# Edge weights of layer 1, made beside the edges of layer 0, stored in rows of their own and loaded by layer 1

## The chip, the cores and the metric

The kernel runs on one core of a Trainium2 chip. Everything is 32-bit float. The metric is the device time in microseconds. A core has five engines that run side by side, each with its own queue of instructions: PE (TensorE, matmuls), ACT (ScalarE), DVE (VectorE), POOL (GpSimd) and SP (SyncE, which only issues DMAs here). They wait for one another through semaphores.

## The reference

Two graph layers follow one another on 50000 nodes with 160 features (64 scalars, 32 vectors of 3) and 25000 edges. A layer maps the features of each edge's source node, multiplies them with weights made from the edge's own attributes, sums the results by target node, maps them once more, and adds a residual and a layer norm. Cut to the parts that matter:

```
def layer0(x, a, src, dst, edge_attr_4, edge_attr_64):
    hid = silu(edge_attr_64 @ fc_w1 / 8)
    w = hid @ fc_w2 / 8                       # 25000 x 224
    es, ev = h_s[src], h_v[src]               # lin1 of x, gathered
    mid = products of w, es, ev, edge_attr_4
    agg = segment_sum(mid, dst)
    ...
def layer1(x, a, edge_attr_16, edge_attr_4, src, dst):
    h = silu(edge_attr_16 @ (Wfc1 / 4))
    w = h @ (Wfc2 / 8)                        # 25000 x 192
    ...
x = layernorm(x + layer0(x, node_vec1, src, dst, edge_attr_4, edge_attr_64))
x = layernorm(x + layer1(x, node_vec1, edge_attr_16, edge_attr_4, src, dst))
```

The `w` of layer 1 depends on `edge_attr_16` and weights alone, not on layer 0.

## The kernel before

The kernel has four stages: edges of layer 0, nodes of layer 0, edges of layer 1, nodes of layer 1. In an edge stage the edges go in 98 pairs of tiles (256 edges a pair), in a node stage the nodes go in 98 groups of 512. The edge sums are added to a table in DRAM by indirect DMAs of POOL (scatters, L500), and source rows come by indirect DMAs of POOL (gathers, L483).

Each engine has its own program for a stage. `run_stages` gives each a list of steps with a lag, and in round i a step with lag n works on pair i - n, in the order of the list. So the order on an engine is written out by hand. In layer 0's edges:

- PE: first_map (lag 1), hidden (0), edge_weights (1), turn_x (0), second_map (3), turn_mid (2), sum_pair (5).
- ACT: copy_z (0), copy_h (1), hidden_act (0), copy_xT (0), copy_message (3), copy_midT (2), copy_sums (5).
- DVE: message vectors (4), scaled attributes (0), comparisons (2), products (1) and the choice of rows (2, 3).
- POOL: gather(k), then scatter(k - 8). A scatter waits for the copied sums of its pair and for the landing of the scatter of the pair before (L493).
- SP: the attributes, the row of targets, and the clearing of layer 1's table, which waits for a scatter to land.

In layer 1's edges PE and ACT also make the self connection of a group of nodes (nodes1a and b, turn1a and b), and SP loads `x1` (320 KB) and stores `base_rows` (320 KB) each round. The edge weights of a pair are made by hidden (L599, attributes times fc1), hidden_act (L763, Silu) and edge_weights (L616 in layer 0, L618 in layer 1), and read out of PSUM by DVE's products.

A wait that matters is in `copy_message`: ACT copies the message of pair j only when PE has summed pair j - 2, since the message buffer has two halves. As copy_message has lag 3 and sum_pair lag 5, it waits for the last matmuls of the same round.

## Time and profile before

| what | value |
|---|---|
| three runs | 2071.84, 2082.07 and 2080.49 us, median 2080.49 |
| the profiled execution | 2057.88 us, its span 2055.1 us |
| busy in the span | PE 1436.3, DVE 1438.8, ACT 1062.9, POOL 1474.8 us |
| mean granted clock of PE | 0.878 of full speed |
| DMA | 439.92 MB, mean 214 GB/s |

The page shows the span in 40 slices of 51 us. In its rows the four stages can be told apart: the two edge stages are slices 3 to 14 and 22 to 34 with 130 to 170 GB/s, the node stages are those with 300 to 400 GB/s, where the DMA engines are busy nearly all the time. The first two slices clear the tables (385 and 430 GB/s). PEclk is the clock that PE was granted, in tenths of full speed; busy shares are tenths as well. An idle gap in an engine's timeline stands in brackets ahead of what ended it; "issue" means that the profile has no name for it.

### The profile page before, as it was taken

Reading aid. Unit: us, or ns where it says so; the run is one execution under the profiler, and the core shown is the slowest. Engines: PE = TensorE matmul, PEld = TensorE weight load, DVE = VectorE, ACT = ScalarE, POOL = GpSimd, SP = SyncE. Lnnn points to the kernel's source line nnn. Section 1 sums busy time; section 2 is a strip of 40 time slices with the busy share of each in tenths; the row PEclk is TensorE's granted clock in tenths of the full one; section 3 lists DMA queues with packets and bytes.
Section 4 is the critical chain, followed back from the end, with each engine's and each line's share of the span. In section 5 each row is a group of like instructions: output and inputs, shape, how many; then the busy total and the mean of one; then the engine's idle time right before and its main releaser. Section 6 shows DMA issues by size and latency. Waiting matters only on the chain.

```text
span 2055.1 us, 48034 instructions
## 1 busy us (share of the span) xinstructions
PE 1436.3 (70%) x10424; PEld 1275.1 (62%) x10424; DVE 1438.8 (70%) x5759; ACT 1062.9 (52%) x3600; POOL 1474.8 (72%) x1923
## 2 busy tenths in 40 slices
PE   5078888788888848888876998999989999300000
PEld 4067777677777737676755888888888888300000
DVE  5067777677777719999983665666656666289998
ACT  3034444444444418999973554554545454146676
POOL 3067888777787647888873777777777777468887
PEclk9589999999999979999997999999999999755555
DMA  9967666676666749999954777777777777499997
GB/s 385 430 151 134 133 137 136 135 132 136 136 135 134 178 101 340 339 337 338 340 208 138 166 167 166 167 170 167 164 162 170 161 169 162 80 362 402 400 399 294
DMA packets 253883, 439.92 MB, mean 214 GB/s; under 512 B 33424, under 2 KB 131152, under 8 KB 250576
## 3 DMA queue, kind: packets, MB, share of 16 engines
q1 hardware_dynamic: 152304, 311.47, 45.1%
q0 software_dynamic: 75264, 67.79, 24.3%
q10 hardware_dynamic: 26208, 59.65, 7.5%
q14 instruction: 91, 0.75, 0.1%
q8 instruction: 16, 0.26, 0.0%
HBM read 235.50 MB, written 203.27 MB: 214 GB/s over the span
## 4 chain that ended last, share of the span: by engine, by line
PE 26%; issue 21%; POOL 13%; ACT 13%; DVE 9%; DMA 6%; SPq 4%; another core or an unknown queue 3%; ACTq 3%; DVEq 1%; POOLq 0%
ACT y L845 9%; POOL table L500 7%; POOL xg L483 5%; DVE stats L1081 3%; SPq L374 3%; DMA table<-sums,row_all 3%; PE ps L679 3%; DVE res L1042 3%; PE ps L660 2%; PE ps L641 2%; PE ps L627 2%; PE ps L643 2%; ACTq L857 2%; PE ps L669 2%
## 5 line engine op out<-in xcount | busy, mean ns | idle before, releaser
L500 POOL DMA_INDIRECT table<-sums,row_all x392 | 630.9, 1609 | 316.4 <-issue 131.2
L782 ACT COPY msg<-ps 128x192 f32<-128x192 f32 (+1 forms) x196 | 57.4, 293 | 680.9 <-PE ps L660 495.8
L845 ACT ACTIVATE y<-res,norm 128x160 f32<-128x160 f32 x756 | 330.3, 507 | 125.8 <-POOL norm L536 69.0
L991 DVE SCALAR_TENSOR_TENSOR x1g<-ps,a_all,x1g 128x160 f32<-128x160 f32 x392 | 132.3, 379 | 200.2 <-PE ps L680 95.3
L483 POOL DMA_INDIRECT xg<-in_x_rows,src_all x196 | 201.8, 1029 | 59.6 <-issue 58.7
L483 POOL DMA_INDIRECT xg<-x_rows,src_all x196 | 195.8, 999 | 64.3 <-issue 58.5
L641 PE MATMUL ps<-weights,midT 128*128 128x128 f32 (+1 forms) x784 | 164.0, 293 | 86.9 <-DVE msg L951 84.8
L946 DVE TENSOR_TENSOR pe<-ps,ea_all 128x192 f32<-128x192 f32 x196 | 69.8, 356 | 185.1 <-ACT msg L782 99.8
L1081 DVE BATCH_NORM_STATS2 stats<-res 128x6 f32<-128x160 f32 x784 | 196.0, 311 | 3.8 <-issue 0.3
L641 PEld LDWEIGHTS ps<-weights,midT 128*128 128x128 f32 x784 | 127.2, 204 | 94.9 <-issue 87.7
L534 POOL TENSOR_TENSOR half_rstd<-var,minus_half 128x8 f32<-128x8 f32 x98 | 165.0, 1683 | 14.2
L643 PE MATMUL ps<-weights,midT 128*128 128x96 f32 x784 | 154.9, 281 | 0.0
L714 PE MATMUL ps<-weights,xzT 128*128 128x160 f32 x784 | 134.0, 313 | 17.7 <-DVE tab L1018 17.7
L591 PE MATMUL ps<-ident,xg 128*128 128x128 f32 x392 | 88.6, 309 | 70.3 <-ACT xz L769 40.2
L679 PEld LDWEIGHTS ps<-weights,xzT 128*128 128x128 f32 x784 | 108.7, 193 | 46.0 <-issue 31.0
L599 PE MATMUL ps<-attrT,weights 128*128 128x128 f32 x392 | 91.5, 316 | 64.4 <-DMA attrT<-in_attrT 43.9
L835 ACT ACTIVATE res<-tab,a_all 128x64 f32<-128x64 f32 x392 | 104.5, 336 | 52.7 <-DVE tab L1018 36.5
L607 PE MATMUL ps<-weights,xgT 128*128 128x128 f32 x784 | 122.4, 280 | 9.2 <-ACT xgT L776 4.7
L679 PE MATMUL ps<-weights,xzT 128*128 128x128 f32 x784 | 122.8, 279 | 8.4 <-issue 3.8
L643 PEld LDWEIGHTS ps<-weights,midT 128*128 128x128 f32 x784 | 128.1, 205 | 0.0
L627 PE MATMUL ps<-ident,mid 128*128 128x128 f32 x784 | 126.7, 287 | 0.0
L714 PEld LDWEIGHTS ps<-weights,xzT 128*128 128x128 f32 x784 | 110.5, 191 | 24.7 <-DMA xzT<-in_xzT 17.9
(115 smaller groups left out, 4465.4 us busy)
## 6 DMA issues: line engine op xcount, KB each, us to landing
tab<-table SPq DMA_DIRECT2D x98, 384.0 KB, 5.0
table<-zeros SPq DMA_DIRECT2D x24, 1536.0 KB
table<-zeros SPq DMA_DIRECT2D x98, 324.0 KB
tab<-table SPq DMA_DIRECT2D x98, 324.0 KB, 5.4
xzT<-in_xzT SPq DMA_DIRECT2D x98, 320.0 KB, 4.9
x1g<-x_rows SPq DMA_DIRECT2D x98, 320.0 KB
base_rows<-x1g SPq DMA_DIRECT2D x98, 320.0 KB
x1g<-base_rows SPq DMA_DIRECT2D x98, 320.0 KB, 4.9
```

The source lines that it names most:

```text
L483: pool.indirect_dma_start(out=xg[j % RING][:, t, 0:width], out_offset=None, in_=rows, in_offset=bass.IndirectOffsetOnAxis(ap=src_all[:, at ...
L500: pool.indirect_dma_start(out=table[l], out_offset=bass.IndirectOffsetOnAxis(ap=row_all[:, at:at + 1], axis=0), in_=sums[j % 4][:, t, 0:W] ...
L534: tt(half_rstd[:, :], var4[:, :], minus_half[:, :], ALU.pow).then_inc(s_rstd, 2)
L607: mm(h_ps[:, t, 0:M], xgT[u][:, t, :], lin1_m[l][:, :], start=True, stop=True)
L627: last = turn(midT_ps[:, 2 * c + t, :], mid[u][:, t, c * P:(c + 1) * P], ident[:, :])
L641: mm(o_ps[l][:, t, 0:SO + V], midT[u][:, t, :], mapA[l][:, :], start=t == 0, stop=not L["cross"], skip_group_check=True)
L643: last = mm(o_ps[l][:, t, SO + V:SO + 4 * V], midT[u][:, 2 + t, :], mapB[l][:, :], start=False, stop=not L["cross"], skip_group_check=True)
L679: mm(n1_ps[:, t, 0:M], xT[v][:, q], self_m[1][:, :], start=True, stop=True)
L714: mm(o[:, t, 0:160], xT[u][:, t * P:(t + 1) * P], self_m[0][:, :], start=True, stop=True)
L845: last = nc.scalar.activation(y[u][:, t, :], res[u][:, t, :], ACT.Identity, scale=rstd[u][:, t:t + 1], bias=shift[u][:, t:t + 1])
L991: last = stt(x1g[v][:, 2 * b + t, :], n1_ps[:, t, :], a, x1g[v][:, 2 * b + t, :], ALU.mult, ALU.add)
L1081: last = nc.vector.bn_stats(stats[u][:, t, :], res[u][:, t, :])
```

## The change

Layer 1's edge weights are now made in layer 0's edge stage, pair by pair. PE gets a matmul of the 16 attributes (`hid1T_ps`) at the head of turn_x and two matmuls for the weights at the head of edge_weights. ACT gets hidden1_act (Silu) and copy_weights1 (PSUM to SBUF, lag 2, right behind copy_z). SP loads both sets of attributes in layer 0 and stores each pair's weights, 128 x 384 floats, to `w1_rows` in DRAM. In layer 1, hidden, hidden_act and edge_weights are gone, and SP loads the weights of each pair in the place where it loaded the attributes; DVE's products wait for that load. Buffers of the node stages (`tab`, `y`) hold the new tiles, and the clearing of attrT on DVE between the layers is gone.

```diff
+        w1_rows = dram("w1_rows", (NP * P, 2 * 192))
...
+        w1_made, w1_read = [[flat(tab2[h + u // 4][:, :, :])[:, u % 4 * 384:(u % 4 + 1) * 384].rearrange("p (t c) -> p t c", t=2)
+                             for u in range(RING)] for h in (0, 2)]
...
+                def store_weights1(j, m, u):
+
+                    wait_count(sp, s_w1store[u], landed(j - 4, u % 4, 4))
+                    sp.sem_inc(s_sptick, 1)
+                    sp.wait_ge(s_w1, j + 1)
+                    sp.sem_inc(s_sptick, 1)
+                    sp.dma_start(w1_rows[bass.ds(m * P, P), :], w1_made[u].rearrange("p t c -> p (t c)")).then_inc(s_w1store[u], 16)
+
+                def load_weights1(j, m, u):
+
+                    wait_count(sp, s_mid, j - 7)
+                    sp.sem_inc(s_sptick, 1)
+                    wait_count(sp, s_w1load[u], landed(j - 4, first_of(u % 4, 4), 4))
+                    sp.sem_inc(s_sptick, 1)
+                    sp.dma_start(w1_read[u].rearrange("p t c -> p (t c)"), w1_rows[bass.ds(m * P, P), :]).then_inc(s_w1load[u], 16)
...
                 if l == 1:
-                    sp.wait_ge(s_attr0, 1)
                     for u in range(4):
                         sp.wait_ge(s_store[u], stored(NG, u))
-                run_stages(sp, base, NP, 10, [(0, load_attr), (0, load_dst_row)] +
-                           ([(0, clear_table0), (8, clear_table1)] if l == 0 else [(4, store_base), (0, load_x1)]), RING)
+                if l == 0:
+                    run_stages(sp, 0, NP, 10, [(0, load_attr), (0, load_dst_row), (0, clear_table0), (5, store_weights1),
+                                               (8, clear_table1)], RING)
+                    for u in range(4):
+                        sp.wait_ge(s_w1store[u], stored(NP, u))
+                else:
+                    run_stages(sp, NP, NP, 10, [(0, load_weights1), (0, load_dst_row), (4, store_base), (0, load_x1)], RING)
...
+                    if l == 0:
+                        pe.wait_ge(s_attr[u], landed(j, u, RING, 32))
+                        wait_count(pe, s_hid1sb, j)
+                        mm(hid1T_ps, fc1[1][0:2 * LAYERS[1]["R"], :], attr1T[u], start=True, stop=True).then_inc(s_hid1, 1)
...
                     wait_count(pe, s_mid, j)
-                    if l == 0:
-                        for t in range(2):
-                            q = slice(t * H, (t + 1) * H)
-                            last = mm(w_ps[0][:, t, :], hidT[u][q, :], fc2[0][q, :], start=True, stop=True)
-                    else:
-                        last = mm(w_ps[1].rearrange("p t c -> p (t c)"), hidT[u][:, :], fc2[1][:, :], start=True, stop=True)
+                    pe.wait_ge(s_hid1sb, j + 1)
+                    wait_count(pe, s_w1, j)
+                    for t in range(2):
+                        mm(w1_ps[:, t, :], hid1T[u], fc2[1][:, t * 192:(t + 1) * 192], start=True, stop=True)
+                    for t in range(2):
+                        q = slice(t * H, (t + 1) * H)
+                        last = mm(w_ps[:, t, :], hidT[u][q, :], fc2[0][q, :], start=True, stop=True)
                     last.then_inc(s_wd, 1)
...
+                def hidden1_act(j, m, u):
+
+                    act.wait_ge(s_hid1, j + 1)
+                    act.wait_ge(s_xgT, j + 1)
+                    wait_count(act, s_wd, j - 1)
+                    nc.scalar.activation(hid1T[u], hid1T_ps, ACT.Silu).then_inc(s_hid1sb, 1)
+
+                def copy_weights1(j, m, u):
+
+                    act.wait_ge(s_mid, j + 1)
+                    wait_count(act, s_w1store[u], landed(j - RING, u % 4, 4))
+                    copy(w1_made[u], w1_ps).then_inc(s_w1, 1)
...
-                    dve.wait_ge(s_wd, j + 1)
+                    if l == 0:
+                        dve.wait_ge(s_wd, j + 1)
+                    else:
+                        dve.wait_ge(s_w1load[u], landed(j, first_of(u % 4, 4), 4))
```

The instructions themselves, first PE in the edge stage of layer 0, from the head of a round (L607, first_map) to the head of second_map. Before (`hidT` is the hidden layer, `xg` the gathered rows, `midT` the turned products):

```order
L607 MATMUL ps<-weights,xgT 128x128 [waits hidden_copied,h_copied,xg_turned_copied]
L607 MATMUL ps<-weights,xgT 128x128
L608 MATMUL ps<-weights,xgT 128x2x32
L599 MATMUL ps<-attrT,weights 128x128 [waits hidden_copied,attr_loaded0]
L616 MATMUL ps<-weights,hidT 128x224 [waits products_ready]
L616 MATMUL ps<-weights,hidT 128x224
L591 MATMUL ps<-ident,xg 128x128 [waits xg_turned_copied,z_gathered_together,rows_gathered0]
L591 MATMUL ps<-ident,xg 128x128
L592 MATMUL ps<-ident,xz 64x128
L641 MATMUL ps<-weights,midT 128x128 [waits message_vectors_ready,message_scalars_ready,products_turned_copied]
```

After (line numbers have moved: first_map is L653, hidden L644, turn_x L636; `y` holds the hidden layer of layer 1 in L662 and its attributes in L634; L662 are the new weights, L665 the old ones):

```order
L653 MATMUL ps<-weights,xgT 128x128 [waits hidden_copied,h_copied,xg_turned_copied]
L653 MATMUL ps<-weights,xgT 128x128
L654 MATMUL ps<-weights,xgT 128x2x32
L644 MATMUL ps<-attrT,weights 128x128 [waits hidden_copied,attr_loaded0]
L662 MATMUL ps<-weights,y 128x192 [waits edge_weights1_copied,hidden1_copied,products_ready]
L662 MATMUL ps<-weights,y 128x192
L665 MATMUL ps<-weights,hidT 128x224 x2
L634 MATMUL ps<-y,weights 128x128 [waits attr_loaded0,xg_turned_copied,hidden1_copied,z_gathered_together,rows_gathered0]
L636 MATMUL ps<-ident,xg 128x128 x2
L637 MATMUL ps<-ident,xz 64x128
L688 MATMUL ps<-weights,midT 128x128 [waits message_vectors_ready,message_scalars_ready,products_turned_copied]
```

Three matmuls stand in the round more, and the first of the edge weights waits for `edge_weights1_copied`, ahead of turn_x.

ACT in the edge stage of layer 0, a round from copy_message on. Before (`msg` is the message, `sums` the pair's sums, `xz` the part of the gathered rows that is brought together):

```order
L782 COPY msg_1<-ps 128x2x96 [waits pair_summed,second_map_done]
L788 COPY midT<-ps 128x512 [waits second_map_done,products_turned]
L790 COPY midT<-ps 96x256
L797 COPY sums<-ps 128x384 [waits pair_summed]
L769 COPY xz<-xg 128x64 [waits xg_turned,rows_gathered1]
L755 COPY hs<-ps 128x2x160 [waits products_ready,hidden_done,h_done]
L757 COPY hs<-ps 128x2x64
L763 ACTIVATE hidT<-ps 128x128 [waits edge_weights_done,hidden_done]
L775 COPY xgT<-ps 128x256 [waits h_done,xg_turned]
```

After (L823 is copy_weights1, into the buffer `tab`; L817 is hidden1_act):

```order
L842 COPY msg_0<-ps 128x2x96 [waits pair_summed,second_map_done]
L848 COPY midT<-ps 128x512 [waits second_map_done,products_turned]
L850 COPY midT<-ps 96x256
L857 COPY sums<-ps 128x384 [waits pair_summed]
L829 COPY xz<-xg 128x64 [waits xg_turned,rows_gathered0]
L823 COPY tab<-ps 128x384 [waits products_ready]
L802 COPY hs<-ps 128x2x160 [waits products_ready,hidden_done,h_done]
L804 COPY hs<-ps 128x2x64
L810 ACTIVATE hidT<-ps 128x128 [waits edge_weights_done,hidden_done]
L835 COPY xgT<-ps 128x256 [waits h_done,xg_turned]
L836 COPY xgT<-ps 64x128
L817 ACTIVATE y<-ps 128x128 [waits edge_weights_done,xg_turned,hidden1_done]
```

The copy of the new weights stands between `xz` and `hs`, the second Silu behind the copies of the turned rows.

PE in the edge stage of layer 1, from first_map to turn_x. Before (L618 are the edge weights, L679 and L680 the self connection):

```order
L607 MATMUL ps<-weights,xgT 128x128 [waits hidden_copied,h_copied,xg_turned_copied]
L607 MATMUL ps<-weights,xgT 128x128
L608 MATMUL ps<-weights,xgT 128x2x32
L599 MATMUL ps<-attrT,weights 128x128 [waits hidden_copied,attr_loaded0]
L618 MATMUL ps<-weights,hidT 128x384 [waits products_ready]
L679 MATMUL ps<-weights,xzT 128x128 [waits self_connection_added,nodes_turned_copied]
L679 MATMUL ps<-weights,xzT 128x128
L680 MATMUL ps<-weights,z1T 128x2x32
L591 MATMUL ps<-ident,xg 128x128 [waits xg_turned_copied,z_gathered_together,rows_gathered0]
```

After:

```order
L653 MATMUL ps<-weights,xgT 128x128 [waits h_copied,xg_turned_copied]
L653 MATMUL ps<-weights,xgT 128x128
L654 MATMUL ps<-weights,xgT 128x2x32
L726 MATMUL ps<-weights,xzT 128x128 [waits self_connection_added,nodes_turned_copied]
L726 MATMUL ps<-weights,xzT 128x128
L727 MATMUL ps<-weights,z1T 128x2x32
L636 MATMUL ps<-ident,xg 128x128 [waits xg_turned_copied,z_gathered_together,rows_gathered0]
```

The matmul of the hidden layer and that of the edge weights are gone with their waits; the self connection (now L726) follows first_map.

## Rows read from the trace of the kernel before

**Rows 1.** The page, part 1: engine, busy us (share of the span) and instructions.

```profile
PE 1436.3 (70%) x10424; PEld 1275.1 (62%) x10424; DVE 1438.8 (70%) x5759; ACT 1062.9 (52%) x3600; POOL 1474.8 (72%) x1923
```

**Rows 2.** Stretches: us, engines' busy us, PEclk, DMA share, GB/s.

```profile
108.00:754.00 646.00, 524.43 (x3697) 463.08 (x3697) 452.61 (x2252) 260.98 (x928) 498.50 (x373) 0.93 0.66 132
...
1131.00:1790.00 659.00, 590.21 (x4592) 543.81 (x4591) 399.14 (x1589) 322.01 (x1303) 488.93 (x372) 0.97 0.73 161
1790.00:2055.00 265.00, 0.00 (x0) 0.00 (x0) 233.50 (x896) 165.68 (x378) 200.72 (x541) 0.50 0.95 362
```

**Rows 3.** Timeline of POOL, layer 0: start, us, instruction [idle before].

```profile
403.30 1.63 POOL L500 DMA_INDIRECT table<-sums,row_all  x1 [0.30 <-issue]
...
407.12 1.02 POOL L483 DMA_INDIRECT xg<-in_x_rows,src_all  x1 [0.30 <-issue]
...
409.73 1.62 POOL L500 DMA_INDIRECT table<-sums,row_all  x1 [0.31 <-issue]
```

**Rows 4.** Waits of POOL, 117 to 707: us in total, times, longest.

```profile
POOL table L500 <- issue: 58.4, 172, 0.8
...
POOL table L500 <- ACT sums L797: 3.5, 3, 2.2
POOL table L500 <- DMA table<-sums,row_all: 2.8, 3, 1.1
```

**Rows 5.** Waits of POOL, 1138 to 1740.

```profile
POOL table L500 <- issue: 67.3, 163, 1.2
POOL xg L483 <- issue: 52.7, 173, 0.3
POOL table L500 <- DMA table<-sums,row_all: 19.1, 13, 2.7
POOL table L500 <- ACT sums L797: 1.9, 2, 1.1
```

**Rows 6.** Timeline of PE, layer 0, one round.

```profile
408.18 0.49 PE L660 MATMUL ps<-msg,same 128*128 128x192 f32 x2
...
410.41 0.44 PE L591 MATMUL ps<-ident,xg 128*128 128x128 f32 x2 [0.27 <-issue]
...
410.79 0.39 PE L641 MATMUL ps<-weights,midT 128*128 128x128 f32 x2
...
413.42 0.49 PE L660 MATMUL ps<-msg,same 128*128 128x192 f32 x2
413.74 0.61 PE L607 MATMUL ps<-weights,xgT 128*128 128x128 f32 x4
```

**Rows 7.** Timeline of ACT, layer 0, the same round.

```profile
408.76 0.32 ACT L782 COPY msg<-ps 128x192 f32<-128x192 f32 x1 [2.50 <-issue]
...
409.72 0.50 ACT L797 COPY sums<-ps 128x384 f32<-128x384 f32 x1
410.09 0.26 ACT L769 COPY xz<-xg 128x64 f32<-128x64 f32 x1
```

**Rows 8.** Timeline of PE, then POOL, at the start and end of layer 0's pairs.

```profile
115.01 0.53 PE L660 MATMUL ps<-msg,same 128*128 128x192 f32 x2
...
117.36 1.83 POOL L500 DMA_INDIRECT table<-sums,row_all  x1 [2.22 <-ACT sums L797]
...
728.72 1.56 POOL L500 DMA_INDIRECT table<-sums,row_all  x1 [2.73 <-ACT sums L797]
```

**Rows 9.** Timeline of PE, layer 1.

```profile
1411.46 0.44 PE L599 MATMUL ps<-attrT,weights 128*128 128x128 f32 x2
1411.74 0.81 PE L618 MATMUL ps<-weights,hidT 128*128 128x384 f32 x2
1412.47 0.68 PE L679 MATMUL ps<-weights,xzT 128*128 128x128 f32 x4
```

**Rows 10.** Timeline of POOL, the first scatter of layer 1.

```profile
1130.87 1.62 POOL L500 DMA_INDIRECT table<-sums,row_all  x1 [24.83 <-ACT sums L797]
```

More of the change, by code:

```diff
@@ L205, in program, with flat @@
         small2 = [sb(f"small{h}", [P, 4, 2, T]) for h in range(RING // 2)]
+        def flat(ap):
+            return ap.rearrange("p a b -> p (a b)")
+        w1_made, w1_read = [[flat(tab2[h + u // 4][:, :, :])[:, u % 4 * 384:(u % 4 + 1) * 384].rearrange("p (t c) -> p t c", t=2)
+                             for u in range(RING)] for h in (0, 2)]
+        attr1T = [flat(y[u // 4][:, :, :])[0:2 * LAYERS[1]["R"], u % 4 * P:(u % 4 + 1) * P] for u in range(RING)]
+        hid1T = [flat(y[2][:, :, :])[:, u % 2 * P:(u % 2 + 1) * P] for u in range(RING)]
         W1 = LAYERS[1]["ROW"]
@@ L246, in program @@
         s_attr = [sem(f"attr_loaded{u}") for u in range(RING)]
-        s_attr0 = sem("attr_cleared")
+        s_hid1 = sem("hidden1_done")
+        s_hid1sb = sem("hidden1_copied")
+        s_w1 = sem("edge_weights1_copied")
+        s_w1store = sem4("edge_weights1_stored")
+        s_w1load = sem4("edge_weights1_loaded")
         s_drow = sem4("dst_row_loaded")
@@ L594, in hidden @@
                 def hidden(j, m, u):
-                    pe.wait_ge(s_attr[u], landed(j, u, RING))
+                    pe.wait_ge(s_attr[u], landed(j, u, RING, 32))
                     wait_count(pe, s_hidsb, j)
-                    mm(hidT_ps, fc1[l][:, :], attrT[u][:, :], start=True, stop=True).then_inc(s_hid, 1)
+                    mm(hidT_ps, fc1[0][:, :], attrT[u][:, :], start=True, stop=True).then_inc(s_hid, 1)
                 def first_map(j, m, u):
@@ L604, in first_map @@
                     wait_count(pe, s_hs, j)
-                    pe.wait_ge(s_hidsb, j + 1)
+                    if l == 0:
+                        pe.wait_ge(s_hidsb, j + 1)
                     for t in range(2):
@@ L703, in _ @@
                 else:
-                    run_stages(pe, NP, NP, 10, [(1, first_map), (0, hidden), (1, edge_weights), (2, nodes1a), (0, turn_x),
+                    run_stages(pe, NP, NP, 10, [(1, first_map), (2, nodes1a), (0, turn_x),
                                                 (1, turn1a), (3, second_map), (2, turn_mid), (1, turn1b),
@@ L751, in copy_h @@
                     act.wait_ge(s_h, j + 1)
-                    if not (isinstance(j, int) and j == (l + 1) * NP - 1):
+                    if l == 0 and not (isinstance(j, int) and j == NP - 1):
                         act.wait_ge(s_hid, j + 2)
@@ L820, in _ @@
                 if l == 0:
-                    run_stages(act, 0, NP, 10, [(0, copy_z), (1, copy_h), (0, hidden_act), (0, copy_xT),
-                                                (3, copy_message), (2, copy_midT), (5, copy_sums)], RING)
+                    run_stages(act, 0, NP, 10, [(0, copy_z), (2, copy_weights1), (1, copy_h), (0, hidden_act), (0, copy_xT),
+                                                (0, hidden1_act), (3, copy_message), (2, copy_midT), (5, copy_sums)], RING)
                 else:
-                    run_stages(act, NP, NP, 10, [(0, copy_z), (1, copy_h), (0, hidden_act), (0, copy_xT),
+                    run_stages(act, NP, NP, 10, [(0, copy_z), (1, copy_h), (0, copy_xT),
                                                  (1, copy_nTa), (3, copy_message), (2, copy_midT), (0, copy_z1),
@@ L1006, in _ @@
                         (4, message_vectors), (2, compare), (4, message_sum), (2, add_self_a), (1, products), (2, add_self_b)], RING)
-                if l == 0:
-                    dve.wait_ge(s_hid, NP)
-                    for u in range(RING):
-                        last = nc.vector.memset(attrT[u][:, :], 0.0)
-                    last.then_inc(s_attr0, 1)
                 def add_table(g, m, u):
```

20 lines of the change are left out of this document (14 added, 6 removed).

## The prediction

> **What bounds the kernel now.** The page gives each engine 52 to 72% of the span [rows 1], so I went by stages. The stretches by stage [rows 2] hold four: edges of layer 0 (108 to 754 us), nodes of layer 0, edges of layer 1 (1131 to 1790), nodes of layer 1 (from 1790). The change touches the two edge stages, 98 pairs of tiles each. In both PE is the busiest engine: 524 of 646 us, and 590 of 659 us.
>
> The timeline of POOL says otherwise. In layer 0, POOL runs two scatters, two gathers, two scatters without a stop: 403.30 to 409.73 us is one pair, 6.43 us, and every gap is 0.30 us [rows 3]. So 6.43 us is POOL's own floor for a pair. The waits of POOL tell what comes on top. From 117 to 707 us (89 pairs, 178 scatters) the gaps ahead of scatters sum to 58.4 + 3.5 + 2.8 = 64.7 us; less 178 x 0.30 that is 11.3 us, 0.13 us a pair [rows 4]. From 1138 to 1740 us they sum to 67.3 + 19.1 + 1.9 = 88.3 us, less 53.4 that is 34.9 us, 0.39 us a pair [rows 5]. What makes them longer in layer 1? Gathers wait 0.30 us each (52.7 us in 173), so the turned rows of PE never hold POOL. Copied sums hold it for 1.9 us in 2 cases. What is left is the wait at L493: each scatter waits until the scatter of the pair before has landed, and the 13 longest gaps carry that name, 19.1 us. Gaps filed under "issue" have no named releaser; I read them as the same wait, since they stand only ahead of the first scatter of a pair. So both edge stages run at POOL's queue plus the landing of a scatter, and PE, ACT and DVE have slack.
>
> **What the change does to layer 0.** Per pair PE gets a 128-column matmul (layer 1's hidden layer) and two of 192 columns; ACT gets a Silu and a 384-column copy; SP gets a load of 16 KB and a store of 192 KB. Sum of the busy time is not the question. The question is the ring that PE and ACT form, because the new copy stands in it.
>
> The ring today: copy_message of pair j waits for the sum of pair j-2, so ACT starts its round when PE's last matmul of a round (L660) ends. Call that E. From E = 408.18 + 0.49 = 408.67 ACT runs msg, midT twice, sums, and xz until 410.09 + 0.26 = 410.35 [rows 7]; PE can turn x only then (410.41), is at L641 at 410.79 and ends its next L660 at 413.42 + 0.49 = 413.91 [rows 6]. One turn is 5.24 us, 1.2 us under the 6.43 us of POOL. That is the cover.
>
> The ring after: copy_weights1 stands right behind copy_z on ACT, and edge_weights, which comes before turn_x on PE, now waits for it. A 384-column copy out of PSUM takes 0.50 us (the sums, [rows 7]). From 410.35 it ends at 410.85, and with the 0.06 us from ACT to PE the first new matmul starts 2.24 us behind E. L660 streams 192 columns in 0.32 us (413.42 to the next start at 413.74 [rows 6]); by columns the new pair is 0.64 us, the old edge weights (2 x 224) 0.38, the hidden layer (128) 0.22. Then turn_x 0.38 (410.41 to 410.79) and the unchanged rest 3.12 (410.79 to 413.91). Sum: 2.24 + 0.64 + 0.38 + 0.22 + 0.38 + 3.12 = 6.98, so 7.0 us a turn, over both POOL's 6.43 and the 6.6 it reaches. First map and old hidden layer come ahead of the waiting matmul and stay under ACT's 2.24 us. The ring is the new bound of this stage. DVE isn't: PE wants its products a whole turn after the edge weights that they need. Nor is SP: the store waits for a copy of five pairs back.
>
> What it costs: PE has finished its round 6 at 115.01 + 0.53 = 115.5, and pair 1 is scattered at 117.36, 1.8 us later [rows 8]; there is hardly a lead that could be spent. After: round 98 ends at 115.5 + 92 x 7.0 = 759.5, pair 93 is scattered at 761.3. Before it was 728.72 [rows 8]. The four pairs behind it are scatters alone in both. **Layer 0: +33 us.** Ends: 0, if the copy is hidden and the turn stays under 6.6; with 7.4 us a turn, +70. The latter is PE's part (4.74 us) at the layer's mean granted clock of 0.93 [rows 2], which gives 2.24 + 4.74 / 0.93 = 7.34, rounded up for waits that I don't see. I take 7.0, the sum of the rows. POOL's landing waits lie under the ring then and cost nothing more.
>
> **What it does to layer 1.** PE loses the hidden layer (0.28 us, 1411.46 to 1411.74) and the edge weights (0.73 us, to 1412.47) [rows 9], ACT a Silu. This frees an engine that POOL doesn't wait for, so it gains nothing in the steady state. SP loads 192 KB of weights a pair (128 x 384 x 4 bytes) in place of 16 KB of attributes. 180 thousand bytes in 6.8 us are 26 GB/s more, and all of them share the DMA engines with the scatters whose landing is the bound. Price: layer 0 moves 132 GB/s and waits 0.13 us a pair, layer 1 161 GB/s and 0.39 us [rows 2, 4, 5], 0.26 us for 29 GB/s; so 26 GB/s cost 0.24 us, over 92 pairs **+22 us**. Ends: 0, if the loads fall among the gathers; and the whole time of the load at 362 GB/s, the rate of the last stage [rows 2], 0.5 us a pair, +46 us. I take 22, from the two stages nearest to it. Below nothing only the fill gains: the first scatter waits 24.83 us for sums [rows 10], some four PE rounds shorter by 1 us each, against five weight loads ahead of everything (0.9 MB, 2.5 us): -2 us.
>
> The rest costs nothing: the memsets of attrT that go stood on DVE while the last scatters ran; SP's waits for the last weight stores end long before the last scatter; the DVE wait on the loaded weights has its load issued some three pairs ahead.
>
> **Sum.** 33 + 22 - 2 = +53 us on the profiled execution (span 2055.1, time 2057.9, so 2111). The three runs of before lie at 2071.8 to 2082.1 with a median of 2080.5, 1.1% over that execution; on the median it makes 2133.
>
> **Rivals.**
> - *The layer 0 ring is hidden.* ACT starts copy_weights1 early enough, or matmuls overlap more, and the turn stays under 6.6 us. For it: 0.4 us is all that has to vanish. Against it: ACT does those copies in order behind E. Then only layer 1 counts, 0 to +22: about 2080 to 2101.
> - *PE is the bound of layer 1, and the kernel gets faster.* PE is busy 590 of 659 us there. If a scatter is late because its sums or vectors are, taking 1.0 us from PE's turn lets the pair fall from 6.81 us to POOL's 6.43: 0.38 x 92 = -35 us, -4 in the fill, and if layer 0 hides its part, 2042; it decides when PE releases POOL in more than the 2 waits named in [rows 5]. With layer 0's +33 it ends near 2075. The Trainium skill, "Perfetto Trace Analysis", Identifying the Most-Contended Engine, says to judge TensorE by its LDWEIGHTS busy share and to optimise the most contended engine first. By it layer 1 is TensorE's (543.8 of 659 us, 83%, against POOL's 74% [rows 2]) and this rival is what comes; the gaps of POOL speak against that.
> - *The ring is longer than its rows.* PE falls to the lower of its two clocks (0.93 on average in layer 0), signals from PE come late, and a turn is 7.4 us: +70, and layer 1 as above or worse: 2170 to 2180.
> - *The change doesn't do what it says*, so that weights arrive late and DVE waits in layer 1. SP issues them right behind the x1 load of the round before, so I give it little; it would look like the last case.
>
> **How the numbers follow.** Main case 62% (its own range 2105 to 2165); ring hidden 14%, half of it within 0.5%; PE bound in layer 1 12%, of which 8 faster and 4 near 2075, within 0.5%; longer ring or late weights 12%. 0.5% (10 us) is about what a measurement of this kernel can tell from no change. Faster 0.08, same 0.11, slower 0.81. The range 2082 to 2172 leaves out the faster cases and the worst of the slow ones.
>
> **What would show it.** In layer 0: the first scatters of two pairs 7.0 us apart instead of 6.6, POOL's gaps ahead of a scatter ended by the copied sums, PE idle ahead of the new 192-column matmuls with the ACT copy as releaser, about 1 us a pair, and the stage over 30 us longer. In layer 1: PE busy down by some 95 us, the POOL gaps longer or equal, never shorter. I am wrong on the ring if the distance stays at 6.6 in layer 0, and on layer 1 if it falls toward 6.43 there.

## The result, and the profile after

The changed kernel takes 2177.4 us (median of 4 runs, 2160.53 to 2179.14); the kernel before 2076.2 us (4 runs, 2066.47 to 2082.07). The ratio is 1.047, with a 95% interval from 1.040 to 1.054. The forecast was 2133 us with a range up to 2172. The sign was right; the loss, 101 us, is about twice the 53 that I had summed, and the time lies outside the range. The profiled execution took 2176.4 us, its span 2174.7. Executions over 1.5% above the fastest of the same kernel count as slow, and medians and ratios below leave them out.

Part 1 of the page, and the stretches by stage (us, engines' busy us, PEclk, DMA share, GB/s), answer to [rows 1, 2]:

```profile
PE 1446.2 (67%) x10620; PEld 1303.0 (60%) x10620; DVE 1453.0 (67%) x5751; ACT 1107.0 (51%) x3698; POOL 1481.5 (68%) x1923
```

```profile
110.00:841.00 731.00, 594.26 (x4247) 517.65 (x4247) 458.18 (x2244) 311.22 (x1112) 497.03 (x373) 0.99 0.65 145
1208.00:1909.00 701.00, 535.78 (x4226) 520.72 (x4226) 404.02 (x1587) 313.80 (x1211) 494.82 (x373) 0.93 0.73 175
1909.00:2174.00 265.00, 0.00 (x0) 0.00 (x0) 234.43 (x896) 165.60 (x378) 200.52 (x541) 0.50 0.95 362
```

Measured from the first pair's first scatter to the last pair's, the edges of layer 0 went from 645 to 730 us and those of layer 1 from 659 to 701. The nodes of layer 1 take 265 us in both. Layer 0's stage is the large part. Together they grew by 127 us and the span by 120: the stretch between them (nodes of layer 0 and the fill of layer 1) went from 375.5 to 365.4 us, and in a second trace of the kernel before (before_again) it had 367.2, so it differs without any edit. The timeline of POOL in layer 0 (start, us, instruction [idle before]), two pairs near the ends and one in the middle:

```profile
119.27 1.83 POOL L541 DMA_INDIRECT table<-sums,row_all  x1 [2.58 <-ACT sums L857]
...
403.71 0.98 POOL L524 DMA_INDIRECT xg<-in_x_rows,src_all  x1 [0.30 <-issue]
406.03 1.87 POOL L541 DMA_INDIRECT table<-sums,row_all  x1 [1.33 <-ACT sums L857]
...
812.09 1.71 POOL L541 DMA_INDIRECT table<-sums,row_all  x1 [3.12 <-ACT sums L857]
```

Pair 1 is scattered at 119.27 and pair 93 at 812.09: 692.82 / 92 = 7.53 us a pair, where it had been (728.72 - 117.36) / 92 = 6.65 [rows 8]. The scatter at 406.03 waits 1.33 us instead of 0.30 [rows 3], and the one who ends the wait is ACT's copy of the sums. The waits of POOL from 119 to 810 say so for the whole stage; before, the sums held it 3 times [rows 4]:

```profile
POOL table L541 <- ACT sums L857: 131.7, 92, 4.1
POOL xg L524 <- issue: 53.6, 176, 0.3
POOL table L541 <- issue: 28.0, 92, 0.3
```

So POOL is no longer the bound; the ring of PE and ACT is. One turn of it on PE, which answers to [rows 6]:

```profile
403.72 0.49 PE L707 MATMUL ps<-msg,same 128*128 128x192 f32 x2
...
406.41 0.89 PE L662 MATMUL ps<-weights,y 128*128 128x192 f32 x4 [1.31 <-ACT tab L823]
407.23 0.65 PE L665 MATMUL ps<-weights,hidT 64*128 64x224 f32 x4
407.81 0.48 PE L634 MATMUL ps<-y,weights 32*128 32x128 f32 x2
408.22 0.44 PE L636 MATMUL ps<-ident,xg 128*128 128x128 f32 x2
...
408.61 0.39 PE L688 MATMUL ps<-weights,midT 128*128 128x128 f32 x2
...
411.23 0.49 PE L707 MATMUL ps<-msg,same 128*128 128x192 f32 x2
```

L707 comes back after 411.23 - 403.72 = 7.51 us. PE stands 1.31 us ahead of the new matmuls (L662), held by ACT's copy of the edge weights (L823, "tab"), as forecast. What differs is the length of the groups behind it; the experiments go into that. On ACT, in the same turn and in answer to [rows 7], the copy of the weights sits behind everything of the round before:

```profile
404.30 0.32 ACT L842 COPY msg<-ps 128x192 f32<-128x192 f32 x1 [2.30 <-PE ps L707]
...
405.25 0.49 ACT L857 COPY sums<-ps 128x384 f32<-128x384 f32 x1
405.62 0.26 ACT L829 COPY xz<-xg 128x64 f32<-128x64 f32 x1
405.77 0.50 ACT L823 COPY tab<-ps 128x384 f32<-128x384 f32 x1
```

In layer 1 PE lost its hidden layer and edge weights: busy 590 us before [rows 2], 536 now. POOL got nothing of it. The gaps ahead of its scatters grew (waits of POOL, 1215 to 1860; before, the landing was named for 13 of them [rows 5]):

```profile
POOL table L541 <- DMA table<-sums,row_all: 61.0, 43, 2.3
POOL xg L524 <- issue: 52.7, 173, 0.3
POOL table L541 <- issue: 39.2, 116, 2.0
POOL table L541 <- ACT sums L857: 25.6, 19, 2.7
```

### The profile page after: what moved, and what is told of

Same layout as the page of the kernel before. It is cut to its first block, busy times and chain, and to the rows that moved or that the text cites. A ratio compares the mean times of both kernels' runs of the same rounds, so it can differ in the third digit from the quotient of the medians.

```text
span 2174.7 us, 49822 instructions
## 1 busy us (share of the span) xinstructions
PE 1446.2 (67%) x10620; PEld 1303.0 (60%) x10620; DVE 1453.0 (67%) x5751; ACT 1107.0 (51%) x3698; POOL 1481.5 (68%) x1923
## 4 chain that ended last, share of the span: by engine, by line
PE 32%; ACT 15%; POOL 14%; DMA 14%; issue 12%; DVE 5%; SPq 4%; ACTq 3%; DVEq 0%; POOLq 0%
DMA table<-sums,row_all 8%; POOL table L541 8%; ACT y L905 8%; PE ps L662 4%; DMA xg<-x_rows,src_all 3%; SPq L411 3%; PE ps L688 3%; PE ps L674 3%; PE ps L665 2%; POOL xg L524 2%; PE ps L690 2%; PE ps L636 2%; PE ps L693 2%; ACT sums L857 2%; DVE stats L1138 2%
## 5 line engine op out<-in xcount | busy, mean ns | idle before, releaser
L636 PE MATMUL ps<-ident,xg 128*128 128x128 f32 x392 | 88.8, 310 | 150.0 <-ACT xz L829 147.0
L970 DVE TENSOR_TENSOR prod<-hs,ea_all 128x192 f32<-128x192 f32 x196 | 70.3, 358 | 161.6 <-ACT hs L804 157.4
L835 ACT COPY xgT<-ps 128x256 f32<-128x256 f32 x196 | 73.0, 373 | 204.0 <-PE ps L637 196.7
L662 PE MATMUL ps<-weights,y 128*128 128x192 f32 x392 | 87.7, 347 | 123.6 <-ACT tab L823 123.6
L636 PEld LDWEIGHTS ps<-ident,xg 128*128 128x128 f32 x392 | 40.9, 145 | 175.3 <-ACT xz L829 145.4
L662 PEld LDWEIGHTS ps<-weights,y 128*128 128x128 f32 x392 | 61.6, 190 | 139.2 <-issue 138.6
L726 PE MATMUL ps<-weights,xzT 128*128 128x128 f32 x784 | 129.9, 290 | 0.6 <-DVE x1g L1054 0.6
```

The source lines that it names most:

```text
L636: turn(xgT_ps[:, t, :], xg[u][:, t, 0:M], ident[:, :])
L662: mm(w1_ps[:, t, :], hid1T[u], fc2[1][:, t * 192:(t + 1) * 192], start=True, stop=True)
L726: mm(n1_ps[:, t, 0:M], xT[v][:, q], self_m[1][:, :], start=True, stop=True)
```

## Experiments

Stage lengths of each profiled execution, from the first scatter of the first pair to the first scatter of the last; "us a pair" is the mean over pairs 1 to 90 of layer 0. A ratio is against the kernel before on the same chip in the same hours, with its 95% interval; the chips differ, so ratios of different sets are compared with care (sets 2 and 3 ran on the same chip). The kernel before had medians of 2087.1, 2093.7, 2088.3 and 2050.4 us in the four sets.

| kernel | set | layer 0, us (a pair) | layer 1, us | time, us | ratio |
|---|---|---|---|---|---|
| before | first | 645 (6.63) | 659 | 2076.2 | |
| after | first | 730 (7.54) | 701 | 2177.4 | 1.047 [1.040, 1.054] |
| copy_early | 1 | 693 (7.14) | 709 | 2146.8 | 1.026 [1.021, 1.030] |
| l1_load_only | 1 | 644 (6.62) | 718 | 2100.6 | 1.006 [1.003, 1.008] |
| l1_relief_only | 1 | 646 (6.66) | 676 | 2065.8 | 0.990 [0.987, 0.994] |
| l1_traffic_only | 1 | 645 (6.64) | 668 | 2063.6 | 0.988 [0.983, 0.994] |
| before_again | 2 | 641 (6.59) | 700 | 2086.5, one run | |
| early_no_store | 2 | 658 (6.77) | 700 | 2103.2, one run | |
| early_x1_ring8 | 2 | 690 (7.12) | 692 | 2128.2 | 1.017 [1.011, 1.022] |
| before_x1_ring8 | 2 | 642 (6.60) | 675 | 2061.6 | 0.985 [0.980, 0.990] |
| hid_k128 | 3 | 715 (7.37) | 728 | 2189.1, one run | |
| all_k128 | 3 | 714 (7.35) | 683 | 2141.4, one run | |
| early_clear_late | 3 | 656 (6.72) | 692 | 2112.6 | 1.018 [1.011, 1.024] |
| layer0_only | 3 | 735 (7.58) | 710 | 2185.6 | 1.046 [1.044, 1.048] |
| hid_beside | 4 | 696 (7.18) | 665 | 2117.4 | 1.033 [1.029, 1.037] |
| fixed_all | 4 | 658 (6.77) | 687 | 2092.3 and 2100.7 | |
| before_clear_ring8 | 4 | 656 (6.77) | 655 | 2066.7 | 1.007 [1.005, 1.010] |
| load_ring8 | 4 | 643 (6.63) | 689 | 2090.5 | 1.020 [1.017, 1.023] |

### Where the ring is closed: copy_early

```diff
-[(0, copy_z), (2, copy_weights1), (1, copy_h), (0, hidden_act), (0, copy_xT), (0, hidden1_act), (3, copy_message), ...
+[(0, copy_z), (1, copy_h), (0, hidden_act), (0, copy_xT), (0, hidden1_act), (1, copy_weights1), (3, copy_message), ...
```

> The changed kernel with one step of ACT moved in layer 0: copy_weights1 now stands ahead of copy_message and takes the pair of one round before (lag 1), where ACT sat idle 2.3 us; nothing else differs. Ring theory (the changed layer 0 turns at 7.51 us because the copy stands between PE's last matmul and the new matmuls): PE's idle 1.31 us ahead of the new matmuls goes, a turn needs 7.51 - 1.31 = 6.2 us, and POOL's 6.43 plus landing waits bounds again, 6.55 to 6.7 us a pair; the stage falls from 730 us to about 645, the kernel from 2177 to about 2092. Rival, PE's added work alone is too long or DVE's products come late: 7.0 us or more a pair, kernel above 2130.

PE's wait for the copy is gone from the list, and the stage falls from 730 to 693 us. So the place of that copy on ACT made the ring. But the pair stays at 7.14 us, not 6.6, and the kernel at 2146.8 us, where I had expected about 2092. These are the numbers of the rival in the expectation, but not for its reason: something else stood behind the copy. The waits of PE and of SP's queue, 130 to 700:

```profile
PE ps L644 <- DMA y<-in_attrT: 49.3, 43, 2.5
```

```profile
SPq L418 <- DMA table<-sums,row_all: 317.6, 80, 5.3
```

PE now waits for the loads of the attributes in 43 rounds, and SP, which issues them, stands in 80 of 80 rounds at L418, where it waits for the landing of a scatter eight pairs back before it clears table rows for layer 1. Before the change it stood there 17 times in the same window:

```profile
SPq L381 <- DMA table<-sums,row_all: 76.6, 17, 5.0
```

In the changed kernel SP is held at the same place (130 to 700), but PE's only named wait there is the one for the copy (98.0 us in 75 rounds), and none for attributes:

```profile
SPq L418 <- DMA table<-sums,row_all: 324.0, 76, 5.3
```

Two readings were left: the new store of 192 KB lies on the scatter and takes its DMA time, or SP's round is held and the attributes come late.

### Store or held round: early_no_store, early_clear_late

```diff
 # early_no_store: copy_early, and
-(0, clear_table0), (5, store_weights1), (8, clear_table1)], RING)
+(0, clear_table0), (8, clear_table1)], RING)
 # and layer 1 loads its weights from the input xzT
 # early_clear_late: copy_early, and
-(8, clear_table1)], RING)
+(10, clear_table1)], RING)
```

> As the kernel with the early copy, without the stores of the weights in layer 0 (layer 1 loads rows of an input in the same packets). Bytes theory of layer 0's rest: the early copy left 7.08 us a pair because the 192 KB store falls on the first 2 us of a scatter and delays its landing; without it the pair takes 6.6 to 6.7 us and the stage 645 to 655 us. Rival, attributes come late (two loads a pair, PE waits for them 49 us): it stays at 7.0 or above.

> copy_early with the clearing of layer 1's table ten pairs behind instead of eight, so that SyncE no longer waits for the landing of a scatter in each round before it can issue the next loads and the store. Theory A (the store of 192 KB lies on the scatter and takes DMA time from it, 0.35 us a pair, wherever SyncE's round is held): the pair stays near 7.1 us, the stage within 10 us of copy_early's 693, total within 0.5% of it (2147). Theory B (SyncE's round is held by the landing wait, the attributes come late, and PE's waits for them set the 7.1): PE's waits on the attribute loads vanish and the pair falls to 6.8 or less, the stage to 665, the total to about 2118.

Without the store the pair takes 6.77 us and the stage 658 (a little over the expected 6.7 and 655), which both readings allow: SP has a transfer less to issue in the held round. early_clear_late keeps the store and moves only the wait: 6.72 us a pair, and PE no longer waits for attributes. What is left of SP's and of PE's waits (130 to 700):

```profile
SPq L400 <- DVE same L1025: 272.9, 84, 5.8
SPq L418 <- DMA table<-sums,row_all: 16.0, 24, 2.3
```

```profile
PE ps L688 <- DVE msg L1014: 28.0, 10, 3.4
PE ps L634 <- ACT xz L829: 1.1, 4, 0.3
```

The held round was the cause. No run takes out the store alone with the clearing ten pairs behind; but 6.72 us with it is only 0.1 over the 6.59 that the kernel before has in a trace of the same chip (before_again), so the bytes can hardly cost more than that. The wait in the issuing queue was worth 0.4 us a pair (7.14 in copy_early, and 7.12 in early_x1_ring8, which has the same layer 0 and ran on the chip of early_clear_late, against 6.72). In the changed kernel itself it lay hidden under the longer ring. The whole time came out at 2112.6 (expected about 2118), though its four runs spread from 2092.57 to 2138.24.

### Why a turn has 7.5 us and not 7.0: hid_k128, all_k128, hid_beside

```diff
 # hid_k128
-mm(hid1T_ps, fc1[1][0:2 * LAYERS[1]["R"], :], attr1T[u], ...)
+mm(hid1T_ps, fc1[1][:, :], attrT[u][:, :], ...)
 # all_k128: this, and
-last = mm(w_ps[:, t, :], hidT[u][q, :], fc2[0][q, :], ...)
+last = mm(w_ps[:, t, :], hidT[u][:, :], fc2[0][:, :], ...)
 # hid_beside: the matmul of hid1T_ps stands in hidden(), not in turn_x()
```

> The changed kernel, with the first-layer matmul for layer 1's hidden layer fed by 128 rows (layer 0's attributes and all 128 rows of the weights) in place of the rows of layer 1's attributes; its load stays. The weights of layer 1 are other numbers then. Theory A (a group of matmuls whose weights have another row count than the group before starts about 0.2 us late, three times a round: 128 to 64, 64 to 32, 32 to 128): one of the three changes goes, and the ring of layer 0 falls from 7.51 us a pair to about 7.3, the stage of edges of layer 0 from 730 us to about 710. Theory B (those matmuls are just slower, whatever their rows): the pair stays at 7.5 and the stage at 730.

> As the run before, and the old edge weights of layer 0 also take all 128 rows of the hidden layer and of the weights instead of 64 (their values are sums of both halves). Theory A: no change of the row count is left in the ring, which falls to about 6.95 us a pair, the number that the prediction had by columns; stage about 680 us. Theory B: 7.5 us, stage 730 us.

> The changed kernel with layer 1's hidden-layer matmul issued right behind layer 0's own hidden layer, ahead of the matmul that waits for the copied weights, where PE is idle. Theory A (the ring is what counts, and its length is the sum of the groups' start distances): the group L634 (0.58 us behind the start of L665, 0.41 us to the next) leaves the ring; what stays is one change of row count in its place, so 7.51 - 0.41 to 0.58 = 6.9 to 7.1 us a pair, the stage 675 to 695 us in place of 730, total about 2132 to 2145. Theory B (the added PE work counts by its sum, wherever it stands): 7.5 us and 730 us.

The same part of a turn in the timelines of PE, hid_k128 and then all_k128:

```profile
406.99 0.89 PE L662 MATMUL ps<-weights,y 128*128 128x192 f32 x4 [1.31 <-ACT tab L823]
407.81 0.65 PE L665 MATMUL ps<-weights,hidT 64*128 64x224 f32 x4
408.39 0.49 PE L634 MATMUL ps<-attrT,weights 128*128 128x128 f32 x2
408.71 0.38 PE L636 MATMUL ps<-ident,xg 128*128 128x128 f32 x2
```

```profile
406.88 0.89 PE L662 MATMUL ps<-weights,y 128*128 128x192 f32 x4 [1.31 <-ACT tab L823]
407.61 0.92 PE L665 MATMUL ps<-weights,hidT 128*128 128x224 f32 x4
408.37 0.38 PE L634 MATMUL ps<-attrT,weights 128*128 128x128 f32 x2
408.59 0.38 PE L636 MATMUL ps<-ident,xg 128*128 128x128 f32 x2
```

In hid_k128 the pair takes 7.37 us and the stage 715, between the two theories and nearer to A (7.3 and 710). One turn of PE is 7.36 us there and 7.35 in all_k128 (from one L707 to the next).

One more piece can be read from copy_early, where PE comes to L662 without the wait for the copy and the row counts are those of the changed kernel:

```profile
508.96 0.82 PE L662 MATMUL ps<-weights,y 128*128 128x192 f32 x4
509.71 0.65 PE L665 MATMUL ps<-weights,hidT 64*128 64x224 f32 x4
```

L662 to L665 is 0.75 us here and 0.82 where PE has stood idle before it. Of the 0.18 us that this term had too little, 0.07 go with the start out of an idle gap and 0.09 with the row count (all_k128).

hid_beside takes the group L634 off the ring to a place where PE stands idle anyway. Its turn of PE:

```profile
403.70 0.49 PE L705 MATMUL ps<-msg,same 128*128 128x192 f32 x2
...
405.01 0.48 PE L642 MATMUL ps<-y,weights 32*128 32x128 f32 x2
406.39 0.89 PE L660 MATMUL ps<-weights,y 128*128 128x192 f32 x4 [0.90 <-ACT tab L821]
407.21 0.65 PE L663 MATMUL ps<-weights,hidT 64*128 64x224 f32 x4
407.79 0.44 PE L632 MATMUL ps<-ident,xg 128*128 128x128 f32 x2
...
410.80 0.49 PE L705 MATMUL ps<-msg,same 128*128 128x192 f32 x2
```

The turn is 7.10 us: 0.41 less than 7.51. The wait shrinks from 1.31 to 0.90, and not a matmul has gone. The stage is 696 us, 34 less (expected 675 to 695, one over the edge). The time of 2117.4 us is under the expected 2132 to 2145, because on this chip the kernel before took only 2050.4 us; the ratio 1.033 is the fair number, against 1.047.

### What layer 1 gave: layer0_only and the pieces of layer 1

```diff
 # layer0_only, layer 1: makes its weights again and loads none
-run_stages(sp, NP, NP, 10, [(0, load_weights1), (0, load_dst_row), ...
+run_stages(sp, NP, NP, 10, [(0, load_attr), (0, load_dst_row), ...
 # l1_load_only: layer 0 as before the change, layer 1 as after, with
-sp.dma_start(w1_read[u]..., w1_rows[bass.ds(m * P, P), :])
+sp.dma_start(w1_read[u]..., A["xzT"][bass.ds(m, 1), :, 0:384]...)
 # l1_relief_only: the same without load_weights1 and DVE's wait for it
 # l1_traffic_only: the kernel before, and in layer 1 that load beside its own matmuls
```

> Layer 0 of the changed kernel (the weights of layer 1 are made, copied and stored), layer 1 of the kernel before (it makes its own again and loads no weights). Theory A (the loss is layer 0's ring; layer 1's stage, some 700 us in typical executions of the kernel before too, is no longer for the change): total within 15 us of the changed kernel, ratio to the kernel before 1.040 to 1.047. Theory B (layer 1 takes a third of the loss, as the two profiled executions say, 41.7 of 119.6 us): ratio 1.025 to 1.03.

> Layer 0 as before the change (no weights of layer 1 are made), layer 1 as after it: no hidden layer and edge weights on PE and ACT, 192 KB a pair loaded by SP, from rows of an input with the same shape of packets, in place of the stored weights. Both theories of layer 1 expect its stage at 701 us as in the changed kernel (659 before) and the kernel at 2076 + 32 = 2108; a stage near 660 would say that layer 1 got longer through something carried over from layer 0.

> As the kernel with layer 1's loads alone, but without the load: layer 1's products read what lies in the buffer. So layer 1 has the relief of PE and ACT and no added bytes. Bytes theory (the 192 KB loads delay the landing of the scatters): the stage is 659 us or a little less (640 to 659), the kernel 2050 to 2076. Phase theory (a shorter PE round moves the stores and loads of x1 onto the scatters): the stage stays near 700, the kernel near 2108. PE-bound rival of the prediction: stage at 625 to 635, 6.43 us a pair.

> The kernel before, with a load of 192 KB a pair added in layer 1 that DVE's products wait for but don't use; PE and ACT keep all their work. Bytes theory: the stage of layer 1 is about 700 us, the kernel about 2115. Phase theory: about 660 and 2080. If both share it, between.

layer0_only has the whole loss: 1.046 against 1.047, as theory A says. The longer layer 0 is enough to explain the result. In the profiles the two stages of layer 1 differed by 42 us, but layer 0 alone leaves nothing for that. The pieces: relief alone and load alone beside the old matmuls cost nothing (both are even 1% under the kernel before), and both together are at 1.006, 13.5 us. So the load is not a fixed price. Of the stage lengths that I had expected, none came out well: 718 us against 701 with both, 676 for the relief alone, between the 659 of the bytes theory and the 700 of the phase theory, and 668 for the load alone, nearer to the phase theory (660).

### The kernel before isn't one number in layer 1: before_again and the x1 buffers

> The kernel before, once more, for a second trace: its profiled execution took 2057.9 us, most others 2083 to 2098. If the stage of layer 1 isn't settled by the work in it but by how stores and loads fall against the scatters, this trace has layer 0 at 644 us again and layer 1 longer than 659, at 680 to 695, with SP's load of x1 issued nearer to the start of a pair's scatter. If the spread has another cause, every stage is longer by the same share.

The kernel before, unchanged and profiled a second time in set 2, had 700 us in layer 1 and not 659. Layer 0 (641 us) and the nodes of layer 1 (265) are near what they were. The waits of SP's queue from 1420 to 1740, first execution and second:

```profile
SPq L388 <- DMA base_rows<-x1g: 44.1, 16, 4.0
SPq L396 <- DVE x1g L991: 30.3, 26, 2.8
```

```profile
SPq L396 <- DVE x1g L991: 115.1, 44, 4.9
SPq L388 <- DMA base_rows<-x1g: 100.9, 43, 3.2
```

In the long one SP waits in every round, first for DVE's x1g and then (L388) for the landing of an earlier store, and each load goes out right behind it. The changed kernel's layer 1 shows the same pattern (1420 to 1740):

```profile
SPq L433 <- DVE x1g L1054: 107.4, 43, 5.1
SPq L425 <- DMA base_rows<-x1g: 102.8, 43, 3.4
```

So the stage can run in a short or a long manner without an edit, and I had summed on an execution with the short one. The change can have both too. hid_beside has the layer 1 of the changed kernel line for line, with the load, and its stage takes 665 us. SP never waits for x1g there, and POOL hardly for a landing (1420 to 1740):

```profile
SPq L425 <- DMA base_rows<-x1g: 55.8, 15, 4.5
```

```profile
POOL table L541 <- DMA table<-sums,row_all: 3.5, 3, 1.3
```

Like beside like, layer 1 has 659 us before and 665 after in the short manner, 700 and 701 in the long one. These traces are of different chips and one execution each, but most of my 42 us lies between the manners and not between the kernels. The pieces of layer 1 (676 and 668 us) lie in between. To take the second wait away I gave the x1 rows eight buffers instead of four:

```diff
-wait_count(sp, s_bstore[v], landed(g - 4, first_of(v, 4), 4))
+wait_count(sp, s_x1[v], landed(g - 4, first_of(v, 4), 4, 32))
-sp.dma_start(x1g[v][:, :, :]...
+sp.dma_start(x1g[u][:, :, :]...
 # and so wherever x1g is named; the wait on s_bstore goes to store_base
```

> The kernel before with the same eight buffers of x1 and nothing else. Phase theory: the stage of layer 1 falls to 625 to 650 us (6.43 to 6.6 a pair), the kernel 1 to 3% below before. Bytes theory: no difference, 2076 to 2090.

> The kernel with the early copy, and x1 loaded into eight buffers in place of four in layer 1's edges, so that its load no longer waits for the landing of a store of base rows: store, weights, target row and x1 are issued in one go, some 5 to 6 us behind the start of a scatter. Phase theory (what costs is that the loads of x1 and the weights go out 1 to 3 us behind the start of a pair's scatters): layer 1 falls from 7.3 to 7.5 us a pair to 6.5 to 6.8, its stage from 709 to 630 to 665 us, the kernel to 2075 to 2110. Bytes theory alone: the same bytes cost the same, stage 690 to 715, kernel 2130 to 2150.

> l1_load_only (layer 0 as in the kernel before; layer 1 loads weights, from an input, and makes none) with eight buffers for the x1 rows. The weights of layer 1 are other numbers. Theory A (the load costs DMA time, 0.15 to 0.25 us a pair): layer 1 at about 690 us against 675 of before_x1_ring8, total 2071 to 2083. Theory B (what l1_load_only lost against l1_relief_only was only where SyncE's transfers fell): within 0.5% of before_x1_ring8 or faster.

> The kernel before with both mends that apply to it: the clearing of the table ten pairs behind, eight buffers for the x1 rows. Theory A (SyncE's round is no bound of layer 0 there, 6.6 us a pair): within 0.5% of before_x1_ring8, 2061. Theory B (it is): under 2050.

> The change with the copy of the weights moved ahead (copy_early), the clearing of the table ten pairs behind (early_clear_late) and eight buffers for layer 1's x1 rows. Theory A (layer 0's loss is the ring of the copy and SyncE's held round, layer 1's is 10 to 20 us of load): layer 0 at 650 to 660 us, layer 1 at 690, total 2085 to 2100, 1.5% over before_x1_ring8 (2061.6). Theory B (the freed PE of layer 1 pays once the rest is mended): at or under 2061.

before_x1_ring8 ran within 2058.82 to 2063.89, 1.5% under the kernel before on its chip (2093.7), and so under both kernels. But in set 4 the kernel before took 2050.4, under 2061.6 (nine runs, eight of them 2047.96 to 2057.91, one 2087.48), and there before_clear_ring8 was 0.7% slower than it. I didn't run before_x1_ring8 on that chip. With eight buffers the wait at L388 is gone, and layer 1 takes 675 and 655 us: under the long manner, not under the short one. The phase theory had 625 to 650 for it; the 692 us of early_x1_ring8 are in the range of the bytes theory (690 to 715).

With eight buffers the load, with the relief of PE that comes with it, has this price. On the chip of set 2: 692 against 675 us, +16 in unrounded lengths (early_x1_ring8, before_x1_ring8). In set 4: 687 and 689 (fixed_all, load_ring8) against 655, +32 and +33. My term was 22. But with four buffers on the same chip hid_beside does the same load in 665 us, so the 32 belong to the load with eight buffers and not to its bytes alone. load_ring8 came out 8 us over its expected time. fixed_all has 2092.3 and 2100.7 us, as theory A expected (2085 to 2100), but the other two of its four runs took 2130.89 and 2131.88. Even the first two lose to the kernel with the same mends (2066.7 in the same set), by 26 and 34 us: theory B, that PE's relief pays once the rest is mended, has fallen. before_clear_ring8 was expected at 2061 and took 2066.7; the later clearing does nothing for a layer 0 without the store (656 us against the 643 of load_ring8, if anything longer).

## Why the prediction was right or wrong

**The bound of before, and the kind of the new one: right.** Layer 0 ran at POOL's queue and runs now at the ring of PE and ACT; PE is held at L662 by the copy, and POOL by the copied sums (92 gaps). copy_early and hid_beside, which change only the order inside that ring, shorten the stage by 37 and 34 us.

**The length of the ring: the step that failed.** I had 7.0 us, and 7.51 came. The path was right; three terms of its sum were too small. Term by term, each from a start to the next start in the timeline of PE (E is the end of L707: 403.72 + 0.49 = 404.21):

| term | forecast | measured |
|---|---|---|
| ACT's part, E to L662 | 2.24 | 406.41 - 404.21 = 2.20 |
| new edge weights | 0.64 | 407.23 - 406.41 = 0.82 |
| old edge weights | 0.38 | 407.81 - 407.23 = 0.58 |
| hidden layer | 0.22 | 408.22 - 407.81 = 0.41 |
| turned x | 0.38 | 408.61 - 408.22 = 0.39 |
| the rest | 3.12 | 411.23 + 0.49 - 408.61 = 3.11 |
| sum | 6.98 | 7.51 |

All that was copied from a place in the old trace that stayed as it was is right within 0.04 us. The three terms that I worked out by columns are 0.57 us short, and they stand where the row count changes. The all_k128 run shows the hidden layer at exactly 0.22 when its neighbours have the same count. The new edge weights lost 0.09 to the row count and 0.07 to the start out of an idle gap. The old edge weights' 0.20 is the size of the other late starts, but no run parts it from the overlap of its two halves. So the step that failed is pricing a new group of matmuls by its columns. Over 92 pairs 0.5 us is 46 us, and that covers the miss: 33 us forecast for layer 0, 812.09 - 728.72 = 83 us measured to pair 93, and 44 us between the forecast of 2133 and the median. My upper end of 7.4 us rested on a slower clock; the clock did the opposite (0.93 before [rows 2], 0.99 after). The upper bound was too low and for a wrong reason; that its turn of 7.4 us came near to 7.51 is luck.

**The size of layer 1: too large if anything, and on a false ground.** +22 was from bytes, -2 from the fill. l1_load_only, which has the change in layer 1 alone, costs 13.5 us. By subtraction it is less or the same: of the 101 us of the result layer 0's stage has 86, which leaves 15; of hid_beside's 67 us it has 53 (696 against the 643 of load_ring8, whose layer 0 is that of before), which leaves 14; layer0_only leaves 4 (101 less its 97, in another set). With eight buffers it measures +16 and +32. In one pair of profiles it can't be told from the manners of the stage: 659 and 700 us without the change, 665 and 701 with it. That 22 lies among these numbers is no support for the 0.24 us a pair by bytes. What was wrong is to read one profiled execution as the stage's length. That this execution lay 1.1% under the median stood in the prediction, and I didn't ask which stage it came from.

**"POOL's landing waits lie under the ring then and cost nothing more": true for POOL, but incomplete.** The wait at L418 that held SP's round was covered too. "Nor is SP" was right in the changed kernel and would have been wrong in its first repair: copy_early shows 0.4 us a pair.

**PE's relief is worth nothing: not contradicted, but not shown by itself.** The rival "PE is the bound of layer 1" rested on PE's busy share of weight loads. The share of before (83%) fell to 520.72 of 701 us, 74%, and the stage didn't get shorter; with layer 0 untouched (l1_load_only) the kernel was 0.6% slower. PE's busy time fell by 54 us (590.21 to 535.78) and not by the 95 that I had named as a sign; the granted clock fell from 0.97 to 0.93 as well. The Trainium skill's rule ("Perfetto Trace Analysis", Identifying the Most-Contended Engine), by which TensorE should have been relieved first, brought no gain here where the relief came with a load. Relief without any load is 1.0% faster in set 1 (l1_relief_only), but so is the load without relief (l1_traffic_only, 1.2%), so I read both as the manner of the stage. No run has the relief alone with the manner held fixed, and a part of that 1.0% may be PE's.

**What stays open.** What puts layer 1 into the long or the short manner: the executions of one chip mostly agree with each other and those of another differ, and several edits of layer 1 change its length. I have not shown why. Nor is it shown why the load costs 16 us with eight buffers on one chip and 32 on another, or why the four runs of early_clear_late and of fixed_all spread over some 40 us.

## What to carry to other kernels

Write a ring down as start-to-start distances, and for a group of matmuls that is new or has new neighbours take the distance from a place in the trace with the same row counts on both sides, not its columns. When a new instruction waits in the middle of an engine's list, move what doesn't need it ahead of the wait: that alone gave back 34 us here. And before trusting a difference between two profiles of a stage, profile the unchanged kernel twice: a stage whose length depends on where its transfers fall can differ by 6% (659 and 700 us here) without any edit.
